# A graph layer and a mixture of experts on one core: the last two nodes' chains side by side, the third-last moved up, pads after the routes, three row buffers

## The reference

```python
x = x + gnn(layernorm(x))                       # x is (12500, 256), float32
#   msgs = f[src] * edge_weight[:, None]        # 212500 edges, sorted by target
#   agg  = segment_sum(msgs, dst); out = agg @ W.T + b
x = x + ffn(layernorm(x))
#   logits = h @ gate_w + gate_b; idx = argmax(softmax(logits))   # 8 experts
#   each row goes to its expert's queue, up to capacity C
#   y = relu(q @ w1[e] + b1[e]) @ w2[e] + b2[e]                   # 256 -> 1024 -> 256
#   result row = y * probability of the expert (0 beyond capacity)
```

## Time and profile before

| | us |
|---|---|
| median of 3 runs | 2467.34 (2462.58 to 2469.74) |
| the profiled execution | 2467.59 |
| its span in the profile | 2465.7 |

### The profile page before, as it was taken

One profiled execution on the slowest core, in us unless ns is written; L12 is line 12 of the kernel. 1 busy time (PEld: TensorE's weight loads), 2 busy tenths in 40 slices (PEclk: granted clock), 3 DMA queues, 4 the chain that ended last, 5 costly groups with the idle time before them and its releaser, 6 DMA issues.

```text
span 2465.7 us, 35440 instructions
## 1 busy us (share of the span) xinstructions
PE 1823.3 (74%) x9798; PEld 1185.8 (48%) x9798; DVE 1164.4 (47%) x5806; ACT 1099.5 (45%) x2565; POOL 1794.0 (73%) x1873
## 2 busy tenths in 40 slices
PE   2333466666888898777777777776887887787699
PEld 1111233333555565455444544554554555554698
DVE  7767443334454454444444444344544544444332
ACT  5667523333545454344434434343543444453343
POOL 6677777777777677777777777777777777777571
PEclk9999975555988899788888888888988988998799
DMA  6566433335553564445445454544554455556567
GB/s 225 187 210 200 121 105 113 113 112 190 155 156 114 161 214 117 152 118 188 118 116 190 116 188 118 188 117 154 155 190 154 117 191 155 190 156 189 180 237 266
DMA packets 139883, 397.04 MB, mean 161 GB/s; under 512 B 36197, under 2 KB 62821, under 8 KB 129046
## 3 DMA queue, kind: packets, MB, share of 16 engines
q0 software_dynamic: 89712, 244.29, 33.4%
q1 hardware_dynamic: 46276, 137.66, 16.2%
q10 hardware_dynamic: 3698, 12.80, 1.4%
HBM read 498.88 MB, written 42.89 MB: 220 GB/s over the span
## 4 chain that ended last, share of the span: by engine, by line
POOL 52%; issue 19%; PE 13%; DVE 8%; ACT 5%; DMA 1%; SPq 0%; DVEq 0%; POOLq 0%; ACTq 0%
POOL msg L621 49%; PE ps L980 5%; ACT msg L735 3%; POOL rows_by_expert L649 3%; DVE wsl L1136 3%; PE ps L968 2%; PE ps L879 2%; PE ps L870 1%; PE ps L959 1%; DVE wsl L1139 1%; DMA hin<-rows_by_expert 1%; DMA msg<-normed,src_sb 1%; POOL out_x L655 1%; ACT wsl L701 0%; PE ps L950 0%
## 5 line engine op out<-in xcount | busy, mean ns | idle before, releaser
L621 POOL DMA_INDIRECT msg<-normed,src_sb x1462 | 1398.1, 956 | 457.4 <-issue 445.2
L870 PE MATMUL ps<-msg,onehot 128*32 128x256 f32 x3332 | 435.2, 505 | 231.1 <-DMA msg<-normed,src_sb 206.9
L1177 DVE TENSOR_TENSOR aggT<-aggT,ps 128x192 f32 x294 | 104.7, 356 | 879.8 <-PE ps L879 856.1
L980 PE MATMUL ps<-wsl,hmid 128*128 128x256 f32 x1680 | 401.4, 394 | 1.5 <-ACT hmid L791 1.5
L744 ACT COPY pairs<-ps 128x256 f32<-128x256 f32 x294 | 111.4, 379 | 618.5 <-PE ps L870 617.6
L879 PE MATMUL ps<-shift,pairs 128*128 128x96 f32 x1176 | 237.3, 334 | 180.5 <-ACT pairs L744 180.5
L980 PEld LDWEIGHTS ps<-wsl,hmid 128*128 128x128 f32 x1680 | 322.9, 197 | 71.9 <-issue 29.5
L950 PE MATMUL ps<-wsl,hTf 128*128 128x512 f32 x680 | 350.1, 662 | 0.5 <-ACT hTf L777 0.5
L870 PEld LDWEIGHTS ps<-msg,onehot 128*32 128x32 f32 x3332 | 139.7, 128 | 413.1 <-DMA msg<-normed,src_sb 256.8
L879 PEld LDWEIGHTS ps<-shift,pairs 128*128 128x128 f32 x1176 | 191.6, 231 | 246.0 <-ACT pairs L744 242.1
L791 ACT ACTIVATE hmid<-ps,wsl 128x128 f32<-128x128 f32 x840 | 230.5, 381 | 133.3 <-PE ps L968 71.2
(11 more groups left out here) (128 smaller groups left out, 2283.3 us busy)
## 6 DMA issues: line engine op xcount, KB each, us to landing
wsl<-in_wsecond SPq DMA_DIRECT2D x105, 1152.0 KB
wsl<-in_wfirst SPq DMA_DIRECT2D x105, 1028.0 KB
msg<-normed,src_sb POOLq DMA_INDIRECT x1462
xrow<-in_x SPq DMA_DIRECT2D x97, 128.0 KB, 2.3
wsl<-in_x SPq DMA_DIRECT2D x24, 512.0 KB, 4.1
normed<-wsl ACTq DMA_DIRECT2D x24, 512.0 KB, 3.0
hin<-rows_by_expert SPq DMA_DIRECT2D x89, 130.0 KB
msg<-in_x,src_sb POOLq DMA_INDIRECT x204
```

Source lines behind the costliest of these rows:

```text
L621: pool.indirect_dma_start(out=msg[:, m + j, :], out_offset=None, in_=x if t < RAW else ln_dram, in_offset=bass.IndirectOffsetOnAxis(ap=src ...
L870: last = nc.tensor.matmul(ps[h * QWIN:(h + 1) * QWIN, t % 2, 0:D], onehot[:, j, :], msg[:, j, :], start=i == 0, stop=i == QUARTERS[q][h] - 1)
L980: last = nc.tensor.matmul(ps[:, Y, 0:D], hmid[:, c, :], w2_at(v % 2)[:, c, :], start=c == 0, stop=c == FC - 1)
```

## The change

- **Order of a node on ACT.** `node_norm` gets an event of its own (`nn`), which stands after the layer part and `expert_norm` of its third instead of right behind `node_root`. DVE's `node` is cut in two (`x2` and `st`), which follow each other directly except for the last two nodes.
- **Third-last node (95).** Its chain is issued inside thirds 291 to 293, a third earlier than before, and its route stands at the end of third 293.
- **Last two nodes (96, 97).** Each step is issued for both in turn. Node 97 has banks, scratch and buffers of its own (`own(n)`).
- **Pads.** They are written after the route of node 97 instead of after that of 95, 128 rows for each queue instead of 384, and without a bounds instruction and the wait for scatters.
- **Row buffers.** Three instead of two.
- **POOL.** The scatter of node 93 stands before the gathers of thirds 292 and 293 instead of behind them. Behind the last gather stood scatters 93, 94, 14 outputs, scatter 95, 12 outputs, scatter 96, 8 outputs, scatter 97 and the rest; now scatters 94 and 95, 12 outputs, scatters 96 and 97 and the rest.
- The number of visits planned ahead falls from 3 to 2, and `ids` and `fin` lie in the space of arrays that are no longer used.

```diff
-AHEAD = 3
+AHEAD = 2
-PADS = 384
+PADS = 128
+LAST_LAG = 2
+HBUFS = 3
...
-    starts = {t: n for n, t in node_at.items()}
+    starts = {t: n for n, t in node_at.items() if n != c}
...
+            if t == thirds - 1:
+                events.append(("rk", c))
             events.append(("mm", t))
+        if t == thirds - 3:
+            events.append(("gnn", c))
+        if t == thirds - 2:
+            events.append(("tn", c))
...
         if stage[1] is not None:
-            events.append(("x2", stage[1]))
+            events += [("x2", stage[1]), ("st", stage[1])]
...
             once("hl", coming)
             once("hn", coming)
+        if stage[1] is not None:
+            events.append(("nn", stage[1]))
...
         events.append(("turn", t))
+        if t == thirds - 2:
+            events += [("lg", c), ("ra", c)]
         events.append(("add", t))
+        if t == thirds - 1:
+            events.append(("rb", c))
...
-    events += [("gnn", a), ("ra", c), ("rk", c), ("x2", a), ("rb", c), ("pads",)]
...
+    events += [("gnn", a), ("gnn", b), ("x2", a), ("x2", b), ("st", a), ("st", b), ("nn", a), ("nn", b)]
     rest()
-    events += [("gnn", b), ("tn", a)]
     rest()
-    events += [("lg", a), ("ra", a), ("x2", b)]
+    events += [("tn", a), ("tn", b)]
     rest()
-    events += [("rk", a), ("rb", a)]
+    events += [("lg", a), ("lg", b), ("ra", a), ("ra", b)]
     rest()
...
+    events += [("rk", a), ("rk", b), ("rb", a), ("rb", b), ("pads",)]
...
-                elif v >= 2:
-                    sp.wait_ge(s_z, v - 1)
+                elif v >= HBUFS:
+                    sp.wait_ge(s_z, v + 1 - HBUFS)
...
-                    row = sp.snap(sp.value_load(pad_i[0:1, e:e + 1], min_val=0, max_val=ROWS - PADS))
-                    scattered_to(sp, NT - 3)
+                    row = sp.snap(nc.values_load(
+                        pad_i[0:1, e:e + 1], engines=[mybir.EngineType.SP], min_val=0, max_val=ROWS - PADS,
...
-            for n, first in ((NT - 4, 14), (NT - 3, 12), (NT - 2, 8), (NT - 1, V)):
+            for n, first in ((NT - 3, 12), (NT - 2, 0), (NT - 1, V)):
...
                 elif kind == "x2":
                     node_root(key[0])
+                elif kind == "nn":
                     node_norm(key[0])
```

More of the change, by code:

```diff
@@ L77, in schedule_of @@
         node_at[n] = t
-    starts = {t: n for n, t in node_at.items()}
+    assert node_at[c] == thirds - 3 and node_at[c - 1] == thirds - 6
+    starts = {t: n for n, t in node_at.items() if n != c}
     full = visits_after(tiles, experts, tiles - 3)
@@ L127, in schedule_of @@
                 once("hl", v)
-        if stage[4] is not None:
+        if stage[4] is not None and stage[4] != c - 1:
             events.append(("rb", stage[4]))
@@ L134, in schedule_of @@
         if stage[1] is not None:
-            events.append(("x2", stage[1]))
+            events += [("x2", stage[1]), ("st", stage[1])]
+        if t == thirds - 3:
+            events += [("x2", c), ("st", c)]
         part = early
@@ L158, in schedule_of @@
             events.append(("gnn", stage[0]))
+        if t == thirds - 3:
+            events.append(("rb", c - 1))
         for v in plan_at.get(t, ()):
@@ L231, in schedule_of @@
         for v in list(rows):
-            if ("wb", max(v - 2, full - 1)) in seen and ("hl", full - 1) in seen:
+            if ("wb", max(v - 2, full - 1)) in seen and ("hl", full - 1) in seen and ("pads",) in seen:
                 order.append(("hl", v))
@@ L409, in gnn_moe_kernel @@
         s_plan = sem("s_plan")
-        s_hin = [sem(f"s_hin{b}") for b in range(2)]
+        s_hin = [sem(f"s_hin{b}") for b in range(HBUFS)]
         s_last = [sem(f"s_last{b}") for b in range(V - FULL)]
@@ L443, in __call__, with own, x2_bank, tr_bank @@
                 self.wait()
+        def own(n):
+            return 1 if n == NT - 1 else 0
+        def x2_bank(n):
+            return 0 if own(n) else X2
+        def tr_bank(n):
+            return 1 if own(n) else TR
+        def normed_rows(n):
+            return pairs[:, 0, :] if own(n) else hrow[:, :]
+        def turned_rows(n):
+            return pairs[:, 1, :].rearrange("p (k t) -> p k t", k=KD) if own(n) else hTs[:, :, :]
         def rows_of(n):
@@ L576, in pad_queues @@
                 for e in range(E8):
-                    row = sp.snap(sp.value_load(pad_i[0:1, e:e + 1], min_val=0, max_val=ROWS - PADS))
-                    scattered_to(sp, NT - 3)
+                    row = sp.snap(nc.values_load(
+                        pad_i[0:1, e:e + 1], engines=[mybir.EngineType.SP], min_val=0, max_val=ROWS - PADS,
+                        skip_runtime_bounds_check_because="a queue's end lies in its part of the buffer"))
                     sp.dma_start(hbuf[bass.ds(row, PADS), :], pads).then_inc(s_pads, 16)
@@ L714, in node_root @@
                 act.wait_ge(s_mv, n + 1)
-                root(sd[:, :], mv[:, 1:2]).then_inc(s_sd, 1)
+                root(sd[:, own(n):own(n) + 1], mv[:, own(n), 1:2]).then_inc(s_sd, 1)
             def normalize_batch(b):
@@ L747, in node_norm @@
                 act.wait_ge(s_stat, n + 1)
-                if n:
+                if own(n):
+                    act.wait_ge(s_turned, T - 1)
+                elif n:
                     act.wait_ge(s_tr, n)
                 row = xrow[:, n % XBUFS, :]
-                nc.scalar.activation(hrow[:, :], row[:, 0:D], ACT.Identity, bias=row[:, X_NMR:X_NMR + 1],
+                nc.scalar.activation(normed_rows(n), row[:, 0:D], ACT.Identity, bias=row[:, X_NMR:X_NMR + 1],
                                      scale=row[:, X_RSTD:X_RSTD + 1]).then_inc(s_h, 1)
@@ L905, in gnn @@
                 pe.wait_ge(s_added, min(3 * (n + 2), T))
-                if n:
+                if n and not own(n):
                     pe.wait_ge(s_x2, n)
                 for k in range(KD):
-                    last = nc.tensor.matmul(ps[:, X2, 0:D], aggT[:, n * P:(n + 1) * P, k], wg_sb[:, k, :],
+                    last = nc.tensor.matmul(ps[:, x2_bank(n), 0:D], aggT[:, n * P:(n + 1) * P, k], wg_sb[:, k, :],
                                             start=k == 0, stop=k == KD - 1)
@@ L918, in turn_node @@
                 for k in range(KD):
-                    last = nc.tensor.transpose(ps[:, TR, k * P:(k + 1) * P], hrow[:, k * P:(k + 1) * P], ident)
+                    last = nc.tensor.transpose(ps[:, tr_bank(n), k * P:(k + 1) * P],
+                                               normed_rows(n)[:, k * P:(k + 1) * P], ident)
                 last.then_inc(s_tr, 1)
@@ L1250, in route @@
             def route(n):
+                l8, ls, choice, eqr, p8 = eights(n)
+                top, sums, best, rank, scale = scalars(n)
                 row = xrow[:, n % XBUFS, :]
                 dve.wait_ge(s_rank, n + 1)
-                link.mark(dve.tensor_tensor(p8, ps[:, TR, D + E8:D + 2 * E8], seen[:, :], ALU.add))
-                link(dve.tensor_tensor(seen[:, :], seen[:, :], ps[:, TR, D + 2 * E8:D + 3 * E8], ALU.add))
+                link.mark(dve.tensor_tensor(p8, ps[:, tr_bank(n), D + E8:D + 2 * E8], seen[:, :], ALU.add))
+                link(dve.tensor_tensor(seen[:, :], seen[:, :], ps[:, tr_bank(n), D + 2 * E8:D + 3 * E8], ALU.add))
                 link.mark(dve.scalar_tensor_tensor(out=p8, in0=p8, scalar=1.0, in1=choice, op0=ALU.mult, op1=ALU.mult,
```

92 lines of the change are left out of this document (47 added, 45 removed).

## The result

| | before | after |
|---|---|---|
| median | 2467.34 (2458.94 to 2469.74, 5 runs) | 2454.11 (2453.13 to 2454.53, 5 runs) |
| span of the profiled execution | 2465.7 | 2452.4 |
| last gather issued | 2260.16 | 2251.25 |
| from there to layer 2 of visit 87 | 71.1 | 66.75 |
| from the last gather to the end | 205.5 | 201.15 |

The medians differ by 13.2 us (0.54%). The ratio formed from all the runs is 0.9958, with an interval of 0.9945 to 0.9971; it isn't the quotient of the two medians, and puts the gain at 0.42%, some 10.4 us, with 7.2 to 13.6 allowed. The prediction was 2453.0. On another chip, in a run of its own further down, the ratio was 0.9957 and the medians differed by 10.75 us.

A forecast was written before the change was run, and what follows sets the result against it. POOL's gathers were taken to bound the gather phase, then the tail up to the dense stretch of visits. From 2467.59 us, -10.5 - 5.1 + 1.0 = -14.6 gave 2453.0 us, range 2444 to 2464.

The forecast's parts named there:

- Part 1: Catch-up, ACT: copies directly behind the root save 1.04 us per cycle, ending POOL's waits between 800 and 1200: -10.5 us.
- part 2: End of the gather phase: the scatter of node 93 ahead of the last 11 gathers delays the last gather by 1.28 us.
- the step from 17.8 to 16.7 us per cycle: Catch-up, 628.35 to 859.38: PE's cycle shortens by 1.04 us through earlier ACT copies, against the 15.5 us POOL needs.
- the ring: Catch-up: four thirds of gathered rows, which took 19.1 of the 29.6 us that PE fell back behind POOL.
- Part 3: From last gather to dense stretch: layer 2 of visit 87 starts 5.1 us earlier, bounds 8.9 to 0.3 us earlier.
- I take 2286.6, 2.7 later: Start of layer 2 of visit 84, formerly 2283.88, delayed by added ACT and DVE work; bounds 0 and 5 us.
- my bound of 7.8: Landing of visit 88's rows: taken as 5.6 us, at most the 7.8 us seen behind two sets of weights.
- the 2.0 us end: Lower bound on the landing of visit 88's rows, with free queues; the Skill's ring-order rule excluded it.
- Part 4: Last visits: 22 more outputs behind the last scatter compete with weights for DMA, between 0 and +4 us, taken as +1.
- the catch-up waits stay: Rival, catch-up: DVE's scale or a low clock sets the cycle, so POOL waits as before; 2463.5 us, chance 0.14.
- the tail gives nothing: Rival, tail: late visit 84, slow pads and a 7.8 us landing take back all 5.1 us; 2458.1 us, chance 0.14.
- the starved weights: Rival, visits from about 2395 to 2425: 22 more outputs hold up the weights, 28 us; time 2480, chance 0.04.

The follow-up runs named there:

- The swap: Kernel after with the rows of visit 88 issued ahead of that visit's second-layer weights, still behind the eight pads: 2444.46 us, ratio 0.9923 to the kernel before.

## Why the prediction was right

The sum was -10.5 - 5.1 + 1.0 = -14.6 us, and the median came out 1.1 us above the forecast. As a difference it was less good: -13.2 in those medians, -10.4 by the ratio, and -10.75 on the chip on which I ran the kernel after again. The forecast of -0.6% lies just outside the interval of the ratio (-0.29% to -0.55%). The direction, the order of the two parts and their places held; that the total came within 1.1 us is partly luck, because both gains were set too high, a cost was forecast that didn't come, and the runs of the kernel before lay high on that occasion (2467.34, against 2462.81 and 2462.74 on two others).

**Part 1, the order on ACT, held in cause and place.** POOL's five waits went and nothing took their place. The last gather came at 2251.25, forecast near 2251; without the 1.28 us of part 2 that is 10.2 us earlier than before. The edit alone moved it by 10.1 us, and in medians it gave 8.1 alone and 7.9 undone (0.9989 against 0.9957, with intervals that allow 4 to 12). So 10.5 was the upper end, as I had said, and the medians lie some 2 us under it. Wrong was the step from 17.8 to 16.7 us per cycle: measured is about POOL's own 15.5 (189 instructions in 238 us), and PE even waits for gathers. I had counted the shorter gap alone. Transposes and aggregations behind it also ran faster, at a granted clock of 0.97 instead of 0.89, so that PE was busy for 14.1 us per first layer (211.53/15) instead of 15.7 (204.75/13). With the order undone, clock and slow transposes are back; that the clock is the cause isn't shown apart from that, and the last section has a stretch in which the clock and the durations part. The error did no harm, since either cycle keeps PE within the ring. The expected idle of 1.4 us per cycle was 1.26 in nine cycles out of fifteen, 0.72 in one, and in five there was none.

**Part 2** is too small to be seen by itself; the last gather's 2251.25 contains it (2260.16 - 10.5 + 1.28 = 2250.9).

**Part 3, the tail, gave 3.0 us instead of 5.1.** Layer 2 of visit 87 came 13.24 us earlier than before, 10.2 of them from part 1. A second pair of traces, from one chip, gives 2.0: behind the last gather it came 69.51 us with the order alone and 66.19 in the kernel after, of which 1.28 us are the moved scatter. With that 10.2 taken off, my walk puts layer 2 of visits 84 to 87 at 2276.4, 2288.3, 2298.4 and 2316.0, and SP's load of rows 88 at 2308.6. Measured were 2273.51, 2285.65, 2295.22 and 2318.00, and 2307.17. Two steps failed, in opposite directions. "I take 2286.6, 2.7 later" was too late: 2273.51 + 10.2 = 2283.7, no later than before, and just under my lower bound. The choice and route of node 95, whose removal I left unpriced, may have made up for what was added ahead; no run shows it. From there the distances were right (12.1 and 9.6 us for 11.9 and 10.1). The 3 us were then lost in front of row 88: 1.8 us of them by pads that took 8.48 us for 7.6 and by what else stood on SP, and the landing of 9.05 us for 5.6 took the rest and 2 us more. The landing was above my bound of 7.8, and above the 8 us that I had named as a sign of being wrong. I had read that bound off two sets of weights issued 1 and 5 us ahead; eight pads and one set just ahead took longer (8.1 and 9.05). The range of the tail was also added up wrongly: 2.0 and 7.8 us of landing alone give 8.7 and 2.9 us, the bounds of the pads widen that to 10.2 and 0.4, and the bounds of visit 84 aren't in it at all.

The Trainium skill says in "DMA: Bandwidth & Descriptors", section "Queues, rings and completion order", that each DMA engine takes the descriptors of SP's queue in ring order. The swap agrees with it: 3.79 us ahead of the 1152 KB, 8.1 to 9.05 behind them. By its rule the 2.0 us end was out, and so it was.

**Part 4, outputs against weights, cost nothing** instead of 1 us. The DMA share reached 1.00 at 411 GB/s, where I had expected a sum over 1, without a PE gap in any visit (the one of 2.08 us ahead of the last instruction was there before too). POOL caught up at 2412.68. My figures of near 2425 and 2312.4 are on the time axis of before; less 10.2 they are 2415 and 2302.2. The catching up came some 2 us earlier than that: the outputs started at 2297.9, 4.3 us earlier, and 86 of them, not 93, stood behind the last scatter.

Of the rivals, "the catch-up waits stay" is out by POOL's empty row between 800 and 1200, "the tail gives nothing" by those 3.0 us and by the 2.5 us in medians that the change is worth with the order undone (an interval that ends at 0.9998, so barely), and the starved weights by the full PE windows.

## What to carry to other kernels

An engine that is never the bound on average can still hold up the one that is, for a stretch: list the bounding engine's few waits by stretch and ask what stands ahead of the late instruction in its queue. One row load of 130 KB that the next step waits for should be issued ahead of a weight load of 1152 KB that is needed later; that swap of two lines was worth 8 us here, as much as the best edit of the change, though nothing on the slower chip. When one wait is taken out of a chain of issues, measure what is late next before believing the sum: of 14.4 us of wait, moving rows 88 removed 7.5 and halving the pads' issues 4.2, and only 9.9 reached the end.

## What the runs showed of the hardware that I had not expected

**A higher clock worth nothing.** Windows from 400 to 600 us, first of the kernel after, then of the one with rows 88 ahead of the pads:

```profile
400.00:600.00 200.00, 129.38 (x572) 76.43 (x572) 79.71 (x398) 60.61 (x113) 151.76 (x159) 0.51 0.45 136
```

```profile
400.00:600.00 200.00, 129.18 (x572) 76.35 (x572) 79.73 (x397) 60.09 (x112) 151.94 (x158) 0.97 0.44 136
```

The granted clock was 0.51 in one, near the level of 1.2 GHz, and 0.97 in the other, near 2.4 GHz, and PE issued 572 matmuls in both. PE's busy time is the same too, and so is the time of single instructions: a matmul of `gnn` took 647 ns in both, where between 628 and 866 us, at 0.97, it took 388. So this clock column and the durations must be read apart. The kernel with the pads on two queues also showed 0.97 in that stretch, the seven others from the chips of normal time that I read 0.50 to 0.51. Why kernels that differ only at their end got different clocks in the middle isn't settled.

**Chips differ.** The same kernel before took 2467.34, 2462.81 and 2462.74 us on three occasions and 2943.39 on a fourth, where the waits of POOL's gathers had grown from some 40 to 476 us. An edit that gained 8 us on the ones gained nothing on the other.
